# Feed-forward tiles taken in pairs: four low-rank products on four row groups of TensorE, four PSUM banks in a ring

## The chip, the cores and the metric

The kernel runs on one core of a Trainium2 chip. The metric is the device time of one execution in microseconds (us). It works in float32 throughout the stage that is changed.

## The reference, cut to what matters

The kernel computes four blocks on `x` (8 sequences of 100 tokens, width 512), each added to `x`: an alignment of `x` with a context, a mixture of 16 experts, a cross-attention, and a feed-forward block with low-rank experts. Only the last is touched:

```python
# x: (8, 100, 512), Wi: (2048, 512), Wo: (512, 2048), E = 4 experts of rank R = 4, TOP_K = 2
logits = einsum('bsd,ed->bse', x, Wg) + bg
scores = softmax(logits)
topv, topi = top_k(scores, 2)
w = sum(one_hot(topi, E) * topv[..., None], axis=-2)
base = einsum('bsd,fd->bsf', x, Wi)                 # shared by the experts
lora_low = einsum('bsd,erd->bser', x, A)            # 4 numbers for each expert
lora = einsum('bser,efr->bsef', lora_low, B)
h = relu(base[:, :, None, :] + lora)
out = einsum('bse,bsed->bsd', w, einsum('bsef,df->bsed', h, Wo))
```

For each token only its two best experts count, so the kernel forms, for each of 2048 hidden features, `w1*relu(base + lora1) + w2*relu(base + lora2)` and multiplies that by `Wo` once.

## The kernel before, in words

The five engines run their own instruction streams, written out by hand; semaphores (`wait_ge`, `then_inc`) are all that orders them. The last stage is `feed_forward` (from L1939).

**Tiles.** The 800 tokens are two halves of `NT4` = 400 columns, the 2048 features are `FJ` = 16 blocks of 128. A tile `i` of 32 is one block of features for one half: `g, f = i // FJ, i % FJ`. It has one PSUM bank of a ring of three (`bank[i % 3]`). Four more banks (`acc`) hold the output of a half, 512 features x 400 tokens, over 16 tiles. The eighth bank, `bx`, takes the logits at first, and later transposed outputs.

**A tile's steps.**
- `base_x(i)` (L2060): four matmuls of 128x128 weights by 400 columns put `Wi x` into the bank.
- `base(i)` (L2084): a matmul with only 16 contraction rows (partitions 0 to 15 of `Bt` and `lowT`) adds the best expert's low-rank term. `low` holds, for each token, the 16 numbers of `lora_low` with those of other experts set to zero.
- `weigh(i, 0)` on VectorE (L2201): relu of the bank, times the first weight `wb[0]`, into `h1`; it increments `read1`.
- `second(i)` (L2090): waits for `read1` and adds, in the same bank, a product of 16 rows at partitions 32 to 47. Those rows hold the second expert minus the first, so the bank now has the second expert's value.
- `weigh(i, 1)`: relu times `wb[1]` into `h2`; it increments `read2`, which also frees the bank.
- GpSimd adds `h1` and `h2` into `hs` (L2004), and increments `hs_ok`.
- `down(i)` (L2100): waits for `hs_ok`, then four matmuls of 128x128 weights `WoT` by 400 columns add to the four `acc` banks.

**TensorE's order (L2117 to L2129).** Iteration `i` issues `base_x(i)`, `base(i)`, `second(i-1)`, `down(i-2)`. The first three `base_x` are issued ahead of the loop (L2064). When half 0 is done, ScalarE and VectorE copy `acc` to `outT`, and iterations 18 to 21 end with `turn_back` of a sequence each (four transposes into `bx`, L2113). VectorE's `finish` adds that to `x` (L2211), and SyncE stores it. The last four sequences follow the loop.

**Ahead of the loop.** LayerNorm, transposes of `x` (L2037), logits (L2045, the first waits for semaphore `w_in` to reach 64: all small loads, `Bt` among them), softmax and top-2 on VectorE, `low` (L2173), whose completion is `low_ok`. TensorE issues `base_x(0..2)`, then waits for `low_ok`, transposes `low` (L2068), VectorE copies it to `lowT` (L2179), and four products of `ones` with diagonals of weights (L2076) spread the weights over the partitions (`wb`, L2183). The loop waits for all of that. SyncE issues the loads in the order `WgA`, `bg`, `Bt` twice, `Wi`, `WoT` (L1982 to L1987).

Of the kernel before, what the change touches and what calls it, by code (L numbers as in the profile page):

```python
# [9 lines left out]
ALU = mybir.AluOpType  # L10
# [3 lines left out]
B, S, D = 8, 100, 512  # L14
C = 722
P = 128
# [1922 lines left out]
def feed_forward(nc, io, res):  # L1939

    ctx = ExitStack()
    with ctx:
        sb, pb, sem = allocator(nc, ctx)
        x_sb, ident, ones = res["x"], res["ident"], res["ones"]
        Wi, WoT = res["Wmem"][:, :].rearrange("p (k f) -> p k f", f=F), sb("WoT", [P, FJ, D])
        Bt = sb("Bt", [2 * 32, F])
        WgA = sb("WgA", [P, KD, E_L + ER])
        bg = sb("bg", [S, E_L])
        stats, mv, rstd = sb("stats_f", [S, B, 6]), sb("mv_f", [S, B, 2]), sb("rstd_f", [S, B])
# [5 lines left out]
        top, topi, topf = sb("top_f", [S, B, 8]), sb("topi_f", [S, B, 8], U32), sb("topf_f", [S, B, 8])  # L1955
        iota_e = sb("iota_f", [S, E_L])
        hot = [sb(f"hot_f{k}", [S, B, E_L]) for k in range(2)]
        low = sb("low_f", [S, B, 64])
        lowT = sb("lowT", [64, XT])
        wdiag = [sb(f"wdiag{i}", [S, B // 2, S]) for i in range(2)]  # L1960
        wb = [sb(f"wb{k}", [P, XT]) for k in range(2)]
        NT4 = XT // 2
        h1 = [sb(f"h1_{i}", [P, NT4]) for i in range(2)]
        h2 = [sb(f"h2_{i}", [P, NT4]) for i in range(2)]
        hs = [sb(f"hs{i}", [P, NT4]) for i in range(3)]
        outT = [sb(f"outT{k}", [P, NT4]) for k in range(KD)]
        NBK = 3
        bank = [pb(f"bf{i}", [P, 512]) for i in range(NBK)]
        acc = [pb(f"acc{i}", [P, 512]) for i in range(4)]
        bx = pb("bx", [P, 512])  # L1970
        turned = [bx] * 4 + bank + [bx]
        w_in, wi_in, wo_in = sem("wf_in"), sem("wi_in"), sem("wo_in")
        (var_ok, root_ok, xn_ok, t_mm, t_ok, l_mm, sub_ok, exp_ok, low_ok, lt_mm, lt_ok, rep_ok, wb_mm, wb_ok, cs,
         base_mm, read1, d_mm, read2, hs_ok, acc_mm, acc_rd, out_s) = (sem("f_" + n) for n in (
# [56 lines left out]
        def _(pe):  # L2031
# [25 lines left out]
            def base_x(i):  # L2057
                g, f = i // FJ, i % FJ
                for k in range(KD):
                    pe.matmul(bank[i % NBK][:, 0:NT4], Wi[:, k, f * P:(f + 1) * P], xT[:, k, g * NT4:(g + 1) * NT4], start=k == 0, stop=False)  # L2060


            pe.wait_ge(wi_in, 16)
            for i in range(NBK):  # L2064
                base_x(i)
            pe.wait_ge(low_ok, 1)
            for b in range(B):
                ins = pe.transpose(acc[b // 4][0:64, (b % 4) * S:(b % 4 + 1) * S], low[:, b, :], ident[0:S, 0:S])  # L2068
                if b % 4 == 3:
                    ins.then_inc(lt_mm, 1)  # L2070
            for i in range(4):
# [6 lines left out]

            def base(i):
                g, f = i // FJ, i % FJ  # L2080
                if i >= NBK:
                    pe.wait_ge(read2, i - NBK + 1)
                    base_x(i)
                pe.matmul(bank[i % NBK][:, 0:NT4], Bt[0:ER, f * P:(f + 1) * P], lowT[0:ER, g * NT4:(g + 1) * NT4], start=False, stop=True).then_inc(base_mm, 1)  # L2084

            def second(i):

                g, f = i // FJ, i % FJ
                pe.wait_ge(read1, i + 1)
                pe.matmul(bank[i % NBK][:, 0:NT4], Bt[32:32 + ER, f * P:(f + 1) * P], lowT[32:32 + ER, g * NT4:(g + 1) * NT4],  # L2090
                          start=False, stop=True, skip_group_check=True).then_inc(d_mm, 1)

            def down(i):
                g, f = i // FJ, i % FJ
                pe.wait_ge(hs_ok, i + 1)
                if g and f == 0:
                    pe.wait_ge(kept_act, 2)
                    pe.wait_ge(kept_dve, 2)
                for k in range(KD):
                    ins = pe.matmul(acc[k][:, 0:NT4], WoT[:, f, k * P:(k + 1) * P], hs[i % 3][:, :], start=f == 0, stop=f == FJ - 1)  # L2100
# [15 lines left out]
            n = 2 * FJ  # L2116
            for i in range(n + 2):  # L2117
                if i < n:
                    base(i)
                if 1 <= i <= n:  # L2120
                    second(i - 1)
                if i == 2:
                    pe.wait_ge(wo_in, 16)
                if i >= 2:
                    down(i - 2)
                if FJ + 2 <= i < FJ + 6:
                    turn_back(i - FJ - 2)
            for b in range(4, B):
                turn_back(b)  # L2129

        @block.vector
        def _(dve):
# [14 lines left out]
            dve.wait_ge(w_in, 64)  # L2147
# [22 lines left out]
            link(dve.tensor_tensor(hot[1][:, :, :], hot[1][:, :, :], hot[0][:, :, :], ALU.subtract))  # L2170
            for b in range(B):
                for k in range(2):
                    ins = dve.tensor_tensor(low[:, b, 32 * k:32 * k + ER].rearrange("p (e r) -> p e r", r=R_L),  # L2173
                                            lga[:, b, E_L:E_L + ER].rearrange("p (e r) -> p e r", r=R_L),
                                            hot[k][:, b, :].unsqueeze(2).broadcast_to([S, E_L, R_L]), ALU.mult)
            ins.then_inc(low_ok, 1)
            for g in range(2):
                dve.wait_ge(lt_mm, g + 1)
                dve.tensor_copy(lowT[:, g * NT4:(g + 1) * NT4], acc[g][0:64, 0:NT4]).then_inc(lt_ok, 1)  # L2179

            def keep_weights(q):
                dve.wait_ge(wb_mm, q + 1)
# [13 lines left out]
            def weigh(i, k):  # L2196
                g = i // FJ
                dve.wait_ge((base_mm, d_mm)[k], i + 1)
                if i >= 2:
                    dve.wait_ge(hs_ok, i - 1)  # L2200
                dve.scalar_tensor_tensor((h1, h2)[k][i % 2][:, :], bank[i % NBK][:, 0:NT4], 0.0, wb[k][:, g * NT4:(g + 1) * NT4],  # L2201
                                         ALU.max, ALU.mult).then_inc((read1, read2)[k], 1)

            def keep_out(g):
# [8 lines left out]
            n = 2 * FJ  # L2213
            for i in range(n):
                weigh(i, 0)
                if i:
                    weigh(i - 1, 1)
                if i == FJ + 1:
                    keep_out(0)
                if FJ + 2 <= i < FJ + 6:  # L2220
                    finish(i - FJ - 2)
            weigh(n - 1, 1)
            keep_out(1)
            for b in range(4, B):
                finish(b)
# [93 lines left out]
```

## Time and profile before

| | us |
|---|---|
| median of 3 runs | 1273.11 (1272.48 to 1273.22) |
| the profiled execution, its own time | 1273.05 |
| its span in the trace | 1271.4 |
| TensorE matmul busy | 1090.3 (86%) |
| VectorE busy | 468.3 (37%) |
| ScalarE busy | 340.4 (27%) |
| GpSimd busy | 208.9 (16%) |

The profile is of one execution. "PE" is TensorE's matmuls, "PEld" its weight loads, which overlap them; DVE is VectorE, ACT ScalarE, POOL GpSimd, SP SyncE. A float32 matmul leaves two matmul records and two weight loads, so a group of 256 records is 128 matmuls of the code. Durations of neighbouring matmuls overlap: what one costs is read from the distance between the starts.

### The profile page before, as it was taken

Reading aid. Unit: us, or ns where it says so; the run is one execution under the profiler, and the core shown is the slowest. Engines: PE = TensorE matmul, PEld = TensorE weight load, DVE = VectorE, ACT = ScalarE, POOL = GpSimd, SP = SyncE. Lnnn points to the kernel's source line nnn. Section 1 sums busy time; section 2 is a strip of 40 time slices with the busy share of each in tenths; the row PEclk is TensorE's granted clock in tenths of the full one; section 3 lists DMA queues with packets and bytes.
Section 4 is the critical chain, followed back from the end, with each engine's and each line's share of the span. In section 5 each row is a group of like instructions: output and inputs, shape, how many; then the busy total and the mean of one; then the engine's idle time right before and its main releaser. Section 6 shows DMA issues by size and latency. Waiting matters only on the chain. (4 is left out here: it accounts for less than half of the span.)

```text
span 1271.4 us, 16885 instructions
## 1 busy us (share of the span) xinstructions
PE 1090.3 (86%) x5214; PEld 691.4 (54%) x5215; DVE 468.3 (37%) x1700; ACT 340.4 (27%) x804; POOL 208.9 (16%) x315
## 2 busy tenths in 40 slices
PE   5776679946937999999999999498999689999997
PEld 4773234522435777767677777244466364555553
DVE  4746888883560000000000000366455352112212
ACT  4323765770001222222222222223355210000000
POOL 0834031110021221212112112000000001111111
PEclk9897899967957999999999999698999967999999
DMA  8579004128305566776595655600000060000000
GB/s 287 141 164 270 8 1 168 56 93 236 117 13 191 179 199 200 263 259 205 197 320 173 181 173 170 188 8 1 0 2 1 16 261 1 1 1 7 20 1 26
DMA packets 76424, 152.52 MB, mean 120 GB/s; under 512 B 17691, under 2 KB 21915, under 8 KB 75567
## 3 DMA queue, kind: packets, MB, share of 16 engines
q1 hardware_dynamic: 63294, 130.95, 30.2%
q0 software_dynamic: 6928, 17.04, 6.1%
q10 hardware_dynamic: 6144, 3.84, 1.4%
q8 instruction: 27, 0.44, 0.1%
q14 instruction: 31, 0.25, 0.1%
HBM read 131.57 MB, written 20.25 MB: 119 GB/s over the span
## 5 line engine op out<-in xcount | busy, mean ns | idle before, releaser
L1269 ACT ACTIVATE att<-phid,b 128x128 f32<-128x128 f32 x216 | 79.4, 368 | 307.9 <-PE phid L1238 307.9
L1291 DVE TENSOR_TENSOR att<-py,att 128x512 f32<-128x512 f32 x27 | 18.7, 692 | 369.2 <-PE py L1246 369.2
L1238 PEld LDWEIGHTS phid<-tiles,W 128*128 128x128 f32 x896 | 111.5, 192 | 37.4 <-issue 37.4
L1238 PEld LDWEIGHTS phid<-tiles,Wmem 128*128 128x128 f32 x832 | 105.5, 195 | 38.9 <-issue 38.9
L1238 PE MATMUL phid<-tiles,W 128*128 x896 | 114.4, 276 | 1.2 <-issue 0.5
L1238 PE MATMUL phid<-tiles,Wmem 128*128 x832 | 108.3, 279 | 5.5 <-issue 4.5
L1246 PE MATMUL py<-W,att 128*128 128x512 f32 x224 | 110.0, 593 | 0.0
L1246 PE MATMUL py<-Wmem,att 128*128 128x512 f32 x208 | 102.2, 593 | 0.0
L2100 PE MATMUL acc<-hs,WoT 128*128 128x400 f32 x256 | 96.3, 521 | 0.5 <-POOL hs L2004 0.5
L2060 PE MATMUL bf<-xT_f,Wmem 128*128 128x400 f32 x256 | 93.2, 509 | 0.0
L2201 DVE SCALAR_TENSOR_TENSOR h<-bf,wb 128x400 f32<-128x400 f32 x64 | 34.0, 570 | 152.4 <-PE bf L2084 148.0
L2100 PEld LDWEIGHTS acc<-hs,WoT 128*128 128x128 f32 x256 | 47.1, 193 | 48.3 <-issue 20.8
L2060 PEld LDWEIGHTS bf<-xT_f,Wmem 128*128 128x128 f32 x256 | 49.4, 195 | 37.0 <-issue 2.2
L2004 POOL TENSOR_TENSOR hs<-h 128x400 f32<-128x400 f32 x32 | 33.0, 1031 | 210.8 <-DVE h L2201 210.8
L1313 POOL DMA_INDIRECT sum_d<-att,to_row x27 | 43.1, 1596 | 143.7 <-DVE att L1294 143.7
L995 PE MATMUL px<-ctx_rows,cost_mem 128*100 128x512 f32 (+1 forms) x96 | 44.7, 618 | 20.6 <-DVE cost_mem L1053 20.6
L2028 ACT COPY outT<-acc 128x400 f32<-128x400 f32 x4 | 1.8, 495 | 221.9 <-PE acc L2100 221.9
L1418 PE MATMUL ba<-lnT,Wmem 128*128 128x400 f32 x128 | 48.6, 525 | 5.6 <-DVE qT L1624 3.2
L858 DVE TENSOR_TENSOR_SCAN cost_mem<-reach_mem,cost_mem,enter 128x93 bf16<-128x93 bf16 x115 | 47.3, 411 | 11.8
L1621 DVE RECIPROCAL inv<-inv 128x400 f32<-128x400 f32 x16 | 42.4, 2652 | 19.7 <-ACT inv L1548 19.3
L1246 PEld LDWEIGHTS py<-W,att 128*128 128x128 f32 x224 | 36.1, 192 | 13.4 <-issue 13.4
L197 POOL TENSOR_SCALAR Wmem<-slots_row,pos_k 128x128 bf16<-128x128 f32 x48 | 39.7, 847 | 21.5 <-DVE pos_k L132 21.5
(364 smaller groups left out, 1655.1 us busy)
## 6 DMA issues: line engine op xcount, KB each, us to landing
Wmem<-in_W SPq DMA_DIRECT2D x16, 2048.0 KB, 14.0
W<-in_W SPq DMA_DIRECT2D x16, 2048.0 KB, 9.2
cT<-in_ctxT SPq DMA_DIRECT2D x8, 1444.0 KB, 11.7
ctx_rows<-in_ctx SPq DMA_DIRECT2D x8, 1280.0 KB
Wmem<-in_Wkv SPq DMA_DIRECT2D x2, 2048.0 KB, 9.2
att<-in_b SPq DMA_DIRECT2D x16, 256.0 KB, 14.1
Wmem<-in_WiT SPq DMA_DIRECT2D x1, 4096.0 KB
WoT<-in_WoT SPq DMA_DIRECT2D x1, 4096.0 KB
```

The costliest lines, as they stand in the source:

```text
L197: pool.tensor_scalar(sel[:, b, t, :], slots_row[:, :], pos[:, t, b:b + 1], None, ALU.is_equal)
L858: dve.tensor_tensor_scan(walk[:, q, 1:NO], code[:, q, :], enter[:, :], walk[:, q, 0:1], ALU.mult, ALU.max).then_inc(scanned_r, 1)
L995: ins = pe.matmul(px[b % 2][:, :], pathf[0:r, b % NPF * CT + t, :], ctx_rows[0:r, b * CT + t, :], start=t == 0, stop=t == CT - 1)
L1238: ins = pe.matmul(ph[j % NH][:, :], W1[u][:, k, j * P:(j + 1) * P], xgT[:, bass.ds(w, 1), k * P:(k + 1) * P].rearrange("p o t -> p (o t)") ...
L1246: ins = pe.matmul(py[:, :], hT[:, j - 2, :], W2[u][:, j - 2, :], start=j == 2, stop=j == HJ + 1)
L1269: act.activation(hT[:, j, :], ph[j % NH][:, :], ACT.Relu, bias=b1[:, bass.ds((e + u) * HJ + j, 1)]).then_inc(relu_ok, 1)
L1313: pool.indirect_dma_start(out=res["sum_d"], out_offset=bass.IndirectOffsetOnAxis(ap=to_row[:, 0:1], axis=0), in_=y[:, :], in_offset=None, ...
L1418: ins = pe.matmul(qk_b[j % 3][:, 0:NH2], w, lnT[:, k, g * NH2:(g + 1) * NH2], start=k == 0, stop=k == KD - 1)
L1621: link(dve.reciprocal(inv[j % 2][:, :], inv[j % 2][:, :]))
L2060: pe.matmul(bank[i % NBK][:, 0:NT4], Wi[:, k, f * P:(f + 1) * P], xT[:, k, g * NT4:(g + 1) * NT4], start=k == 0, stop=False)
L2100: ins = pe.matmul(acc[k][:, 0:NT4], WoT[:, f, k * P:(k + 1) * P], hs[i % 3][:, :], start=f == 0, stop=f == FJ - 1)
L2201: dve.scalar_tensor_tensor((h1, h2)[k][i % 2][:, :], bank[i % NBK][:, 0:NT4], 0.0, wb[k][:, g * NT4:(g + 1) * NT4], ALU.max, ALU.mult).the ...
```

## The change

Tiles are taken two at a time. Iteration `q` of 18 issues `base_x` of tiles 2q and 2q+1, then four products of 16 rows in a row: `base(2q)`, `base(2q+1)`, `second(2q-2)`, `second(2q-1)`, then `down(2q-4)`, a `turn_back` in iterations 10 to 13, and `down(2q-3)`. An even tile uses partitions 0 and 32 of `Bt` and `lowT`, an odd one 64 and 96, so `Bt`, `low` and `lowT` have four copies of the 16 rows. The ring of banks has four; the fourth is the former `bx`, so `base_x(3)` is issued after `low_ok`, and `turn_back` borrows the ring bank that `weigh(2q-2, 1)` has just read. `h1` and `hs` get four buffers.

```diff
-        Bt = sb("Bt", [2 * 32, F])
+        Bt = sb("Bt", [P, F])
-        low = sb("low_f", [S, B, 64])
-        lowT = sb("lowT", [64, XT])
+        low = sb("low_f", [S, B, P])
+        lowT = sb("lowT", [P, XT])
-        NBK = 3
+        NBK, NPAIR = 4, FJ
+        BACK_AT = FJ // 2 + 2
-        bx = pb("bx", [P, 512])
-        turned = [bx] * 4 + bank + [bx]
+        bx = bank[NBK - 1]
+        turned = [bank[2 * (BACK_AT + b - 1) % NBK] for b in range(B // 2)] + bank
...
-            for i in range(2):
+            for i in range(4):
                 sp.dma_start(Bt[32 * i:32 * i + ER, :], io["Bt"]).then_inc(w_in, 16)
...
-                if i >= 3:
-                    pool.wait_ge(acc_mm, i - 2)
-                pool.tensor_tensor(hs[i % 3][:, :], h1[i % 2][:, :], h2[i % 2][:, :], ALU.add).then_inc(hs_ok, 1)
+                if i >= 4:
+                    pool.wait_ge(acc_mm, i - 3)
+                pool.tensor_tensor(hs[i % 4][:, :], h1[i % 4][:, :], h2[i % 2][:, :], ALU.add).then_inc(hs_ok, 1)
...
-                    pe.wait_ge(w_in, 64)
+                    pe.wait_ge(w_in, 96)
...
-            for i in range(NBK):
+            for i in range(NBK - 1):
                 base_x(i)
             pe.wait_ge(low_ok, 1)
+            base_x(NBK - 1)
             for b in range(B):
-                ins = pe.transpose(acc[b // 4][0:64, (b % 4) * S:(b % 4 + 1) * S], low[:, b, :], ident[0:S, 0:S])
+                ins = pe.transpose(acc[b // 4][:, (b % 4) * S:(b % 4 + 1) * S], low[:, b, :], ident[0:S, 0:S])
...
             def base(i):
                 g, f = i // FJ, i % FJ
-                if i >= NBK:
-                    pe.wait_ge(read2, i - NBK + 1)
-                    base_x(i)
-                pe.matmul(bank[i % NBK][:, 0:NT4], Bt[0:ER, f * P:(f + 1) * P], lowT[0:ER, ...], ...).then_inc(base_mm, 1)
+                r = 64 * (i % 2)
+                pe.matmul(bank[i % NBK][:, 0:NT4], Bt[r:r + ER, f * P:(f + 1) * P], lowT[r:r + ER, ...], ...).then_inc(base_mm, 1)
             def second(i):
+                r = 64 * (i % 2) + 32
                 pe.wait_ge(read1, i + 1)
-                pe.matmul(..., Bt[32:32 + ER, ...], lowT[32:32 + ER, ...], ...).then_inc(d_mm, 1)
+                pe.matmul(..., Bt[r:r + ER, ...], lowT[r:r + ER, ...], ...).then_inc(d_mm, 1)
...
-                if b in (1, 2, 3):
-                    pe.wait_ge(acc_rd, b)
-                if b == B - 1:
-                    pe.wait_ge(acc_rd, 4)
+                if b < B // 2:
+                    pe.wait_ge(read2, 2 * (BACK_AT + b - 1) + 1)
+                if b == B // 2:
+                    pe.wait_ge(acc_rd, B // 2)
...
+            for q in range(NPAIR + 2):
+                pair = (2 * q, 2 * q + 1)
+                if 2 <= q < NPAIR:
+                    if 0 <= q - 1 - BACK_AT < B // 2:
+                        pe.wait_ge(acc_rd, q - BACK_AT)
+                    for i in pair:
+                        pe.wait_ge(read2, i - NBK + 1)
+                        base_x(i)
+                if q < NPAIR:
+                    for i in pair:
+                        base(i)
+                if 1 <= q <= NPAIR:
+                    for i in pair:
+                        second(i - 2)
+                if q == 2:
+                    pe.wait_ge(wo_in, 16)
+                if q >= 2:
+                    down(2 * q - 4)
+                    if 0 <= q - BACK_AT < B // 2:
+                        turn_back(q - BACK_AT)
+                    down(2 * q - 3)
...
             def weigh(i, k):
-                if i >= 2:
-                    dve.wait_ge(hs_ok, i - 1)
+                if i >= (4, 2)[k]:
+                    dve.wait_ge(hs_ok, i - (3, 1)[k])
...
+            for q in range(NPAIR + 1):
+                if q:
+                    weigh(2 * q - 2, 1)
+                    weigh(2 * q - 1, 1)
+                if q < NPAIR:
+                    weigh(2 * q, 0)
+                    weigh(2 * q + 1, 0)
+                if q == BACK_AT - 1:
+                    keep_out(0)
+                if 0 <= q - BACK_AT < B // 2:
+                    finish(q - BACK_AT)
```

The loop's old body, which the last two groups of lines replace, is at L2116 to L2127 and L2213 to L2222. The operations that build `low` on VectorE stay 16, and each now writes 32 numbers for a token, not 16.

## Rows read from the trace of the kernel before

**Rows 1.** The page: busy time of each engine, and TensorE's granted clock in 40 slices.

```profile
PE 1090.3 (86%) x5214; PEld 691.4 (54%) x5215; DVE 468.3 (37%) x1700; ACT 340.4 (27%) x804; POOL 208.9 (16%) x315
PEclk9897899967957999999999999698999967999999
```

**Rows 2.** Stretches: length, then PE, PEld, DVE, ACT, POOL busy, clock, DMA.

```profile
1072.71:1254.84 182.13, 182.13 (x577) 92.50 (x575) 33.38 (x62) 0.89 (x2) 28.87 (x28) 1.00 0.02 5
1052.00:1065.50 13.50, 12.30 (x20) 5.48 (x21) 4.68 (x9) 0.00 (x0) 2.05 (x2) 0.50 0.00 0
```

**Rows 3.** TensorE in order of time: start, us, line, operation. One tile of the loop.

```profile
1241.95 2.85 PE L2060 MATMUL bf<-xT_f,Wmem 128*128 128x400 f32 x8
1244.73 0.60 PE L2084 MATMUL bf<-lowT,Bt 16*128 16x400 f32 x1
1244.74 0.60 PE L2090 MATMUL bf<-lowT,Bt 16*128 16x400 f32 x1
1245.17 0.49 PE L2084 MATMUL bf<-lowT,Bt 16*128 16x400 f32 x1
1245.60 2.95 PE L2100 MATMUL acc<-hs,WoT 128*128 128x400 f32 x8
1248.39 2.85 PE L2060 MATMUL bf<-xT_f,Wmem 128*128 128x400 f32 x8
```

**Rows 4.** The same view: the end of the loop, and what follows.

```profile
1252.05 2.95 PE L2100 MATMUL acc<-hs,WoT 128*128 128x400 f32 x8
1254.93 0.93 PE L2090 MATMUL bf<-lowT,Bt 16*128 16x400 f32 x2
1255.79 5.64 PE L2100 MATMUL acc<-hs,WoT 128*128 128x400 f32 x16
1262.67 1.49 PE L2113 MATMUL bf<-ident,outT 128*100 128x128 f32 x12 [1.24 <-DVE outT L2207]
```

**Rows 5.** Groups by line from 1060 us on: busy, mean ns; idle before.

```profile
L2004 POOL TENSOR_TENSOR hs<-h 128x400 f32<-128x400 f32 x32 | 33.0, 1031 | 210.8 <-DVE h L2201 210.8
L2201 DVE SCALAR_TENSOR_TENSOR h<-bf,wb 128x400 f32<-128x400 f32 x62 | 32.8, 570 | 149.9 <-PE bf L2084 145.4 <-PE bf L2090 3.2 <-POOL hs L2004 1.2
```

**Rows 6.** All engines in order of time: a transposed sequence inside the loop.

```profile
1166.55 2.95 PE L2100 MATMUL acc<-hs,WoT 128*128 128x400 f32 x8
1169.34 0.60 PE L2113 MATMUL bx<-ident,outT 128*100 128x128 f32 x4
1169.78 2.85 PE L2060 MATMUL bf<-xT_f,Wmem 128*128 128x400 f32 x8
```

**Rows 7.** All engines in order of time: the start of the loop.

```profile
1055.41 3.03 PE L2084 MATMUL bf<-lowT,Bt 16*128 16x400 f32 x4 [0.67 <-DVE wb L2183]
1057.22 0.57 DVE L2201 SCALAR_TENSOR_TENSOR h<-bf,wb 128x400 f32<-128x400 f32 x1 [1.86 <-PE bf L2084]
1057.85 1.03 PE L2090 MATMUL bf<-lowT,Bt 16*128 16x400 f32 x1
1059.59 0.57 DVE L2201 SCALAR_TENSOR_TENSOR h<-bf,wb 128x400 f32<-128x400 f32 x1 [0.53 <-PE bf L2090]
1061.42 5.02 PE L2100 MATMUL acc<-hs,WoT 128*128 128x400 f32 x8 [0.54 <-POOL hs L2004]
1066.27 2.85 PE L2060 MATMUL bf<-xT_f,Wmem 128*128 128x400 f32 x8
```

**Rows 8.** All engines in order of time: ahead of the loop.

```profile
1037.24 10.54 PE L2060 MATMUL bf<-xT_f,Wmem 128*128 128x400 f32 x24
1042.11 1.46 DVE L2173 TENSOR_TENSOR low_f<-lga,hot_f 100x16 f32<-100x16 f32 x16
1047.61 0.85 PE L2068 MATMUL acc<-ident,low_f 100*64 100x100 f32 x8
```

**Rows 9.** The loads: SyncE's issue of `Bt`, and the wait that ended with it.

```profile
1014.05 1.20 SPq L1985 DMA_DIRECT2D Bt<-in_Bt  x2
PEld bx L2045 <- issue: 2.9, 1, 2.9
```

More of the change, by code:

```diff
@@ L1962, in feed_forward @@
         NT4 = XT // 2
-        h1 = [sb(f"h1_{i}", [P, NT4]) for i in range(2)]
+        h1 = [sb(f"h1_{i}", [P, NT4]) for i in range(4)]
         h2 = [sb(f"h2_{i}", [P, NT4]) for i in range(2)]
-        hs = [sb(f"hs{i}", [P, NT4]) for i in range(3)]
+        hs = [sb(f"hs{i}", [P, NT4]) for i in range(4)]
         outT = [sb(f"outT{k}", [P, NT4]) for k in range(KD)]
-        NBK = 3
+        NBK, NPAIR = 4, FJ
+        BACK_AT = FJ // 2 + 2
         bank = [pb(f"bf{i}", [P, 512]) for i in range(NBK)]
         acc = [pb(f"acc{i}", [P, 512]) for i in range(4)]
-        bx = pb("bx", [P, 512])
-        turned = [bx] * 4 + bank + [bx]
+        bx = bank[NBK - 1]
+        turned = [bank[2 * (BACK_AT + b - 1) % NBK] for b in range(B // 2)] + bank
         w_in, wi_in, wo_in = sem("wf_in"), sem("wi_in"), sem("wo_in")
@@ L2080, in base @@
                 g, f = i // FJ, i % FJ
-                if i >= NBK:
-                    pe.wait_ge(read2, i - NBK + 1)
-                    base_x(i)
-                pe.matmul(bank[i % NBK][:, 0:NT4], Bt[0:ER, f * P:(f + 1) * P], lowT[0:ER, g * NT4:(g + 1) * NT4], start=False, stop=True).then_inc(base_mm, 1)
+                r = 64 * (i % 2)
+                pe.matmul(bank[i % NBK][:, 0:NT4], Bt[r:r + ER, f * P:(f + 1) * P], lowT[r:r + ER, g * NT4:(g + 1) * NT4],
+                          start=False, stop=True).then_inc(base_mm, 1)
             def second(i):
                 g, f = i // FJ, i % FJ
+                r = 64 * (i % 2) + 32
                 pe.wait_ge(read1, i + 1)
-                pe.matmul(bank[i % NBK][:, 0:NT4], Bt[32:32 + ER, f * P:(f + 1) * P], lowT[32:32 + ER, g * NT4:(g + 1) * NT4],
+                pe.matmul(bank[i % NBK][:, 0:NT4], Bt[r:r + ER, f * P:(f + 1) * P], lowT[r:r + ER, g * NT4:(g + 1) * NT4],
                           start=False, stop=True, skip_group_check=True).then_inc(d_mm, 1)
@@ L2099, in down @@
                 for k in range(KD):
-                    ins = pe.matmul(acc[k][:, 0:NT4], WoT[:, f, k * P:(k + 1) * P], hs[i % 3][:, :], start=f == 0, stop=f == FJ - 1)
+                    ins = pe.matmul(acc[k][:, 0:NT4], WoT[:, f, k * P:(k + 1) * P], hs[i % 4][:, :], start=f == 0, stop=f == FJ - 1)
                 ins.then_inc(acc_mm, 1)
@@ L2114, in turn_back @@
                 ins.then_inc(back_mm, 1)
[L2116 to L2122, printed above, removed]
-                    pe.wait_ge(wo_in, 16)
-                if i >= 2:
[L2125 to L2128, printed above, removed]
+            for q in range(NPAIR + 2):
[13 more added lines that the diff above has]
+                if q == 2:
+                    pe.wait_ge(wo_in, 16)
+                if q >= 2:
[3 more added lines that the diff above has]
+                    down(2 * q - 3)
+            for b in range(B // 2, B):
                 turn_back(b)
@@ L2146, in _ @@
             dve.wait_ge(l_mm, B)
-            dve.wait_ge(w_in, 64)
+            dve.wait_ge(w_in, 96)
             dve.wait_ge(cs, 3)
@@ L2172, in _ @@
                 for k in range(2):
-                    ins = dve.tensor_tensor(low[:, b, 32 * k:32 * k + ER].rearrange("p (e r) -> p e r", r=R_L),
-                                            lga[:, b, E_L:E_L + ER].rearrange("p (e r) -> p e r", r=R_L),
-                                            hot[k][:, b, :].unsqueeze(2).broadcast_to([S, E_L, R_L]), ALU.mult)
+                    ins = dve.tensor_tensor(low[:, b, :].rearrange("p (u k c) -> p u k c", u=2, k=2)[:, :, k, 0:ER].rearrange("p u (e r) -> p u e r", r=R_L),
+                                            lga[:, b, E_L:E_L + ER].rearrange("p (e r) -> p e r", r=R_L).unsqueeze(1).broadcast_to([S, 2, E_L, R_L]),
+                                            hot[k][:, b, :].unsqueeze(1).unsqueeze(3).broadcast_to([S, 2, E_L, R_L]), ALU.mult)
             ins.then_inc(low_ok, 1)
@@ L2178, in _ @@
                 dve.wait_ge(lt_mm, g + 1)
-                dve.tensor_copy(lowT[:, g * NT4:(g + 1) * NT4], acc[g][0:64, 0:NT4]).then_inc(lt_ok, 1)
+                dve.tensor_copy(lowT[:, g * NT4:(g + 1) * NT4], acc[g][:, 0:NT4]).then_inc(lt_ok, 1)
             def keep_weights(q):
@@ L2198, in weigh @@
                 dve.wait_ge((base_mm, d_mm)[k], i + 1)
-                if i >= 2:
-                    dve.wait_ge(hs_ok, i - 1)
-                dve.scalar_tensor_tensor((h1, h2)[k][i % 2][:, :], bank[i % NBK][:, 0:NT4], 0.0, wb[k][:, g * NT4:(g + 1) * NT4],
+                if i >= (4, 2)[k]:
+                    dve.wait_ge(hs_ok, i - (3, 1)[k])
+                dve.scalar_tensor_tensor((h1[i % 4], h2[i % 2])[k][:, :], bank[i % NBK][:, 0:NT4], 0.0, wb[k][:, g * NT4:(g + 1) * NT4],
                                          ALU.max, ALU.mult).then_inc((read1, read2)[k], 1)
@@ L2211, in finish @@
                 dve.tensor_tensor(x_sb[:, b, :], x_sb[:, b, :], turned[b][0:S, :], ALU.add).then_inc(acc_rd, 1)
[L2213 to L2218, printed above, removed]
+            for q in range(NPAIR + 1):
[6 more added lines that the diff above has]
+                if q == BACK_AT - 1:
                     keep_out(0)
-                if FJ + 2 <= i < FJ + 6:
-                    finish(i - FJ - 2)
-            weigh(n - 1, 1)
+                if 0 <= q - BACK_AT < B // 2:
+                    finish(q - BACK_AT)
             keep_out(1)
```

## The prediction

> **What bounds the kernel now.** I read the page first: TensorE is busy for 1090.3 of 1271.4 us, no other engine for more than 468.3 [rows 1]. That is an average over four stages, so I went to the stretch of the changed loop. From 1072.71 to 1254.84 us TensorE's matmuls cover all 182.13 us at a granted clock of 1.00 (the 2.4 GHz level), VectorE works 33.38, GpSimd 28.87 [rows 2]. Those two wait for TensorE: VectorE's two readings of a tile are 0.57 us each, GpSimd's sum is 1.03, and nearly all of their idle time ended with TensorE's product (145.4 of VectorE's 149.9 us) [rows 5]. So the loop lasts as long as TensorE's matmuls, and only what shortens TensorE's own sequence counts.
>
> Then I took one tile in order of time, by the distances between starts [rows 3]:
> - four `base_x` matmuls, 1241.95 to 1244.73: 2.78 us
> - the slot of the low-rank products, 1244.73 to 1245.60: 0.87
> - four `down` matmuls, 1245.60 to 1248.39: 2.79
>
> A tile is 6.44 us. In the slot `base(i)` and `second(i-1)` run at once: their first records start 0.01 us apart, though each has a second record 0.44 later. The end of the loop shows what one such product costs when it is alone: `second(31)` starts at 1254.93 and `down(30)` at 1255.79, 0.86 us [rows 4]. One product costs 0.86, two on two row groups 0.87. This pair of rows carries the forecast: the slot is paid per group of products, not per product. Before 1066.27 us the picture differs: TensorE waits for VectorE and GpSimd, and the clock is 0.50, the 1.2 GHz level, from 1052.0 to 1065.5 [rows 2, 7].
>
> **The change part by part.** The full-size matmuls stay as they are, 32 tiles of 4 + 4, and so do the eight `turn_back`. What differs:
>
> *Slots in the loop.* After its start (from `down(0)` on) the kernel before has 29 slots of 0.87 (tiles 3 to 31) and one of 0.86: 26.09 us. After its start (from `base_x(4)` on) the changed one has 14 slots of four products (q = 2 to 15) and one of two (q = 16). At 0.87 each that is 12.18 + 0.86 = 13.04. The gain is 13.05 us. No row shows four products in one slot. Lower bound of such a slot: 0.87, nothing added. Upper bound: four after each other, 4 x 0.86 = 3.44; two by two is 1.74. I take 0.89, by the nearest row: the second product added 0.01, so two more add 0.02. That costs 14 x 0.02 = 0.3.
>
> The row on this is the pair 0.86 against 0.87 [rows 3, 4]. The Trainium skill, TensorE: Matmul & The Clock Gate, section "Measured speedup vs the span model", speaks against it in part: four row tiles of 32 rows gave 3.07 times the speed of one after another, not four. By that an estimated slot is 4 x 0.86 / 3.07 = 1.12 us, 14 x 0.25 = 3.5 us more than 0.87 in each, and the sum would end at 1262.4 us. The trace does not bear that out for two products, and does not show four.
>
> The same page, "The cost: per-tile semaphore tail", puts some 26 ns on each increment, and a slot now has four where it had two. An estimate by it is 14 x 0.05 = 0.7 us more; the trace has the second product's increment within its 0.01 us. I stay with the row.
>
> *Start of the loop.* Before, from the first low-rank product (1055.41) to `down(0)` (1061.42) pass 6.01 us [rows 7]: products with waits for VectorE between them, then GpSimd. After, `base(0)` and `base(1)` run together, and both are ready after 1.81 us (1057.22 less 1055.41); VectorE reads `bank 0` and `bank 1`; `second(0)` starts 0.63 us after the first reading began (1057.85 less 1057.22), and VectorE can read its result 1.74 later (1059.59 less 1057.85), which takes 0.57 and frees bank 0. Sum: 1.81 + 0.63 + 1.74 + 0.57 = 4.75, some 4.8 with the wait's latency, and then `base_x(4)` starts; `base(2)` and `base(3)` lie beside. GpSimd's sum is off the path, as `down(0)` comes only after two `base_x` and a slot. Gain 1.2 us. If the latencies don't overlap so: 0; if the clock were high: up to 2.5.
>
> *base_x(3) moves* ahead of the loop, past the wait for `low_ok` and ahead of the transposes of `low`. `low` is ready at 1043.57 (1042.11 + 1.46), while TensorE is in `base_x(0..2)` until 1047.61 [rows 8], so the new place in the queue causes no wait; it moves the transposes, and with them `lowT`, the weights and the loop's start, by 2.78 us. The loop has one `base_x` less, 2.78. Net 0. The transposes write 128 partitions, not 64, with weight loads twice as wide: they take 0.85 now [rows 8]; I add 0.1, at most 0.85.
>
> *The clock.* `down(0)` takes from 1061.42 to 1066.27, 4.85 us in place of 2.79, at the lower level [rows 7]: 2.06 lost. After, `base_x(4)` starts there instead, equally behind a few us of sparse products, and I take the same loss. TensorE's idle time while the weights are spread is as long as before but 2.8 us later, so the fall and the rise of the clock may come elsewhere. The low stretch was 13.50 us [rows 2] with 4.85 of dense work in it; gone altogether it would give back 2 to 3 us, and as much again in dense work would cost 2.
>
> *Edits I cost at nothing.* VectorE's 16 operations for `low` double in size; they took 1.46 us and have 4.04 of cover (1043.57 to 1047.61) [rows 8]; uncovered at most 1.46. The memset of `low` on GpSimd lies in some 24 us before it is needed. Two more loads of `Bt` stand ahead of `Wi` on SyncE's queue. The issue of two took 1.20 us, and the first logits wait for the loads: the weight loader's idle time before the logits, counted from the end of that wait, was 2.9 us [rows 9], the slack of the `Bt` loads. 1.2 to 1.8 later fits in it; without it the logits slip by at most 1.2. `Wi` and `WoT` follow 1.2 later, with `WoT` first needed 24 us after `base_x(0)`; were `Wi` late, the cost is those 1.2.
>
> *New waits in the loop.* Four readings of VectorE now follow each slot: 4 x 0.57 = 2.3 us, then two sums of GpSimd, 2.1. The bank for `base_x(2q)` is that of tile 2q-4, whose second reading is first in line behind slot q-1, done after some 0.6 us, while TensorE has two `down`, 5.58 us, ahead of it. The bank of 2q+1 follows by 0.6. `hs` has four buffers, and `down` comes 5.6 us and a slot after its sum. A `turn_back` adds 0.44 (1169.34 to 1169.78) before and after [rows 6]. Its new borrowed bank is read 0.6 us behind the slot, and the transposes start 2.79 behind it. `finish` holds the bank until some 3.9 us (2.79 + 0.44 + 0.69), and the next pair needs it at 6.0. Slack 2 us; without it up to 4 x 0.7 = 2.8 lost. Behind a waiting TensorE instruction stands everything, so any such miss is paid in full.
>
> *The tail* from `down(31)` on is the same work: copies, 16 transposes, additions, stores. 0.
>
> Sum: 13.05 + 1.2 - 0.3 - 0.1 = 13.85 us. The profiled execution took 1273.05 us (span 1271.4 and 1.65 around it), 0.06 below the median of 1273.11. Forecast: 1259.2 us, a span of 1257.55.
>
> **The rivals.**
> 1. *Four products only partly together*, some 1.12 us a slot. For: more weight loads and results in the same time than any row shows. Against: the second product's 0.01. 14 x (1.12 - 0.89) = 3.2 less gain: 1262.4 us. This is also what the page's factor gives.
> 2. *Two by two*, which is that the change does not do what it says: a slot of 1.74. For: each product has two records, and eight in flight are not seen. Against: a second record does not hold back the other product now. Slots 14 x 1.74 + 0.86 = 25.2, gain 0.9, with the start and the transposes 2.0: 1271.1 us, no change to tell.
> 3. *One after another.* If TensorE starts a product on a new row group only when the semaphore wait ahead of it has been passed with the array empty, a slot becomes 3.44: 14 x (3.44 - 0.89) = 35.7 more, and 1294.9 us, slower. It decides from a slot of 1.88 on (0.89 + 13.85 / 14). Against: `second` has such a wait now and starts within 0.01 us.
> 4. *Waits on the ring*: one stall in each pair at the bank or at `turn_back`. One of 0.2 us costs 3, 1262; 1 us in every pair would eat all of it. Slacks of 2 to 5 us speak against.
>
> **How the numbers follow.** Forecast 0.78; rival 1 0.09; rival 2 0.04; rival 3 0.03; rival 4 0.06. The forecast's own range is 1256.5 (clock low stretch gone) to 1261.5 (loads late, clock worse). With rivals 1 and most of 4 the range goes to 1263.5 and holds over 8 in 10. A measurement here tells 0.2%, 2.5 us. Faster by more: 0.92; within: 0.04; slower: 0.04.
>
> **What would show it.** In the profile after: four low-rank products that start within 0.05 us of each other, and 0.87 to 0.91 us from the first to `down`; a period of 12.03 us for a pair (2 x 5.57 + 0.89); `base_x(4)` some 4.8 us behind the first product; transposes of `low` at 1050.4; no idle time of TensorE before L2060 or L2113 of the kernel before, in the loop. The forecast is wrong if the slot is above 1.1, if a wait for `read2` or `acc_rd` appears on TensorE, or if the logits wait for `Bt`.

## The result, and the profile after

| | us |
|---|---|
| before, median | 1273.16 (1272.48 to 1274.41, 4 runs) |
| changed, median | 1256.20 (1254.46 to 1259.77, 4 runs) |
| ratio | 0.9869, 95% interval 0.9844 to 0.9895 |
| forecast | 1259.2 (1256.5 to 1263.5) |

The change is faster, as forecast, but by 17.0 us in place of 13.9, and the median lies 0.3 us below the range. The interval of the ratio stands for a gain of 13.4 to 19.9 us, so the medians of these runs alone do not tell by how much the forecast missed. Two later groups of runs of the same two kernels put the gain at 19.2 and 18.6 us, and the traces show where it comes from. The profiled execution took 1257.63 us, its span is 1255.0.

First TensorE in order of time in the changed kernel (start, us, line): a pair of tiles, then the end of the loop. A row group, below, is a block of 32 partitions of `Bt` and `lowT`; the four begin at 0, 32, 64 and 96. This answers to [rows 3, 4].

```profile
1071.06 0.60 PE L2084 MATMUL bf<-lowT,Bt 16*128 16x400 f32 x2
1071.08 0.60 PE L2092 MATMUL bf<-lowT,Bt 16*128 16x400 f32 x2
1071.50 0.50 PE L2084 MATMUL bf<-lowT,Bt 16*128 16x400 f32 x2
1071.52 0.50 PE L2092 MATMUL bf<-lowT,Bt 16*128 16x400 f32 x2
1071.95 5.64 PE L2102 MATMUL acc<-hs,WoT 128*128 128x400 f32 x16
1077.43 5.54 PE L2061 MATMUL bf<-xT_f,Wmem 128*128 128x400 f32 x16
1082.89 0.60 PE L2084 MATMUL bf<-lowT,Bt 16*128 16x400 f32 x2
...
1233.04 0.94 PE L2092 MATMUL bf<-lowT,Bt 16*128 16x400 f32 x4
1233.91 11.01 PE L2102 MATMUL acc<-hs,WoT 128*128 128x400 f32 x32
```

The slot with four products takes 0.89 us (1071.06 to 1071.95), as forecast. But the pair takes 11.83 us (1071.06 to 1082.89), not 12.03: two `down` are 5.48 and two `base_x` 5.46, where twice the durations of before make 5.58 and 5.56. The full-size matmuls did not stay as they were.

Now the way into the loop, all engines in order of time, which answers to [rows 7, 8].

```profile
1039.41 13.20 PE L2061 MATMUL bf<-xT_f,Wmem 128*128 128x400 f32 x32
1052.45 0.85 PE L2070 MATMUL acc<-ident,low_f 100*128 100x100 f32 x8
1056.67 1.91 PE L2078 MATMUL acc<-wdiag,ones 100*128 100x400 f32 x4 [0.48 <-DVE wdiag L2200]
1059.25 1.61 PE L2084 MATMUL bf<-lowT,Bt 16*128 16x400 f32 x8 [0.67 <-DVE wb L2194]
1063.29 7.85 PE L2061 MATMUL bf<-xT_f,Wmem 128*128 128x400 f32 x16 [0.18 <-DVE h L2212]
```

From the first low-rank product to `base_x(4)` pass 4.04 us, forecast 4.75. And the same stretches with their granted clock (last but two of the columns):

```profile
1045.00:1061.00 16.00, 13.48 (x48) 6.82 (x46) 6.90 (x22) 0.00 (x0) 0.00 (x0) 1.00 0.00 1
1061.50:1068.00 6.50, 6.32 (x12) 2.98 (x11) 2.02 (x4) 0.00 (x0) 2.02 (x2) 0.52 0.00 0
1071.06:1233.04 161.98, 161.98 (x561) 86.81 (x560) 32.07 (x62) 0.89 (x2) 28.34 (x28) 1.00 0.02 6
```

The clock stays at the 2.4 GHz level until about 1061, over the products that spread the weights and the first slot; before, it fell at 1052 and stayed low for 13.5 us [rows 2]. Now it is low for some 6.6, two thirds of that under `base_x(4)` and `base_x(5)`, which take 7.77 us (1063.29 to 1071.06) in place of 5.46.

Where the stage begins matters for the comparison. Its first VectorE operation started at 1013.13 us before and at 1015.30 after. The code ahead is the same, and in later profiles that operation falls between 1011.35 and 1016.14 whatever was edited behind it. So spans compare badly, and I use the length of the last stage, from that operation to the end of the span.

```profile
1013.13 1.29 DVE L2138 TENSOR_TENSOR x_res<-x_res,att 100x512 f32<-100x512 f32 x2 [4.47 <-PEq L45]
```

```profile
1015.30 1.29 DVE L2149 TENSOR_TENSOR x_res<-x_res,att 100x512 f32<-100x512 f32 x2 [4.56 <-PEq L45]
```

The first is of before: 1271.4 - 1013.13 = 258.27 us. The second is of after: 1255.0 - 1015.30 = 239.70. The stage gained 18.6 us where the forecast had 13.85. In this execution the stage began 2.2 us later than in that of before, which hides as much of the gain from the spans (16.4 us).

### The profile page after: what moved, and what is told of

The parts are those of the page before. It is cut to its first block and busy times, and to the rows that moved or that the text cites. A ratio compares the mean times of both kernels' runs of the same rounds, so it can differ in the third digit from the quotient of the medians.

```text
span 1255.0 us, 16888 instructions
## 1 busy us (share of the span) xinstructions
PE 1072.4 (85%) x5214; PEld 688.3 (55%) x5215; DVE 466.7 (37%) x1700; ACT 340.8 (27%) x804; POOL 208.2 (17%) x315
## 5 line engine op out<-in xcount | busy, mean ns | idle before, releaser
L2102 PE MATMUL acc<-hs,WoT 128*128 128x400 f32 x256 | 90.6, 505 | 0.0
L1246 PEld LDWEIGHTS py<-W,att 128*128 128x128 f32 x224 | 36.1, 192 | 13.4 <-issue 13.4
L825 DVE TENSOR_TENSOR_SCAN ctx_rows<-ctx_rows,cost_mem 128x46 f32<-128x46 f32 x115 | 37.3, 325 | 12.3 <-DVE ctx_rows L822 0.5
## 6 DMA issues: line engine op xcount, KB each, us to landing
att<-in_b SPq DMA_DIRECT2D x16, 256.0 KB, 14.1
```

The source lines that it names most:

```text
L825: dve.tensor_tensor_scan(reach[:, s + 1, 1:ROW], lower[:, s, :], cost[:, :, s], reach[:, s + 1, 0:1], ALU.min, ALU.add).then_inc(scanned, 1)
L1246: ins = pe.matmul(py[:, :], hT[:, j - 2, :], W2[u][:, j - 2, :], start=j == 2, stop=j == HJ + 1)
```

## The experiments

Of each profile I give the period of a pair of tiles and the length of the last stage ("stage"). The kernel before ran beside each group: 1274.41 us (`again`, `two_visits`, `two_groups`, `idle_fill`), 1274.66 (`no_lowrank`, `one_product`, `full_height`, `late_fourth`), 1275.56 (the last three). It was profiled once, at the start, so a stage of before is always 258.27. A visit is one passage of TensorE to the low-rank products and back. Its edges are the time that it adds to the full-height groups on its two sides, beside the slot itself. Full-height matmuls are those over all 128 contraction rows.

**The changed kernel again, unedited.**

> The changed kernel once more, nothing edited, to see what moves by itself. Every theory: a pair of tiles takes 11.83 us in the loop and a slot of four products 0.87 to 0.89, as in its first profile. The part from the last stage's first VectorE operation to the end is 239.7 us, within 0.3. If the times differ from each other by several us, the difference lies ahead of that stage.

1255.23 us; ratio 0.9856 (0.984 to 0.9873). The pair is 11.83, the stage 1250.5 - 1011.35 = 239.15. That is 0.55 less than in the first profile, more than the 0.3 expected: the four `base_x` ahead of the loop took 12.69 us in place of 13.04, and `base_x(4)` and `base_x(5)` 7.60 in place of 7.77, both with a part of them at the lower clock. The stage began 4 us earlier. So single executions differ by several us for reasons ahead of the stage, and the stage's length repeats to about 0.5.

**Two visits to the low-rank products.**

```diff
-                if q < NPAIR:
-                    for i in pair:
-                        base(i)
                 if 1 <= q <= NPAIR:
                     for i in pair:
                         second(i - 2)
...
                         turn_back(q - BACK_AT)
+                if q < NPAIR:
+                    for i in pair:
+                        base(i)
+                if q >= 2:
                     down(2 * q - 3)
```

> The four products of a pair of tiles are issued at two places: second, second, then down, then base, base, then down. All products, banks and waits stay. Theory A (each passage between full-height matmuls and products of 16 rows costs about 0.1 us beside the slot itself, so a slot costs 0.87 + 0.2): a pair takes 11.83 + 0.87 + 0.2 = 12.9 us, and the kernel 14 x 1.07 = 15 us more than the changed one, 1271. Theory B (the 0.2 us a pair that the change saved beyond the slot belong to the passages between base_x and down, which are also half as many): 11.83 + 0.87 = 12.7 us a pair, 12 us more, 1268.

1270.92 us (ratio to before 0.9977, 0.9967 to 0.9987). TensorE in order of time:

```profile
1079.43 5.54 PE L2061 MATMUL bf<-xT_f,Wmem 128*128 128x400 f32 x16
1084.90 0.94 PE L2092 MATMUL bf<-lowT,Bt 16*128 16x400 f32 x4
1085.77 2.95 PE L2102 MATMUL acc<-hs,WoT 128*128 128x400 f32 x8
1088.65 0.94 PE L2084 MATMUL bf<-lowT,Bt 16*128 16x400 f32 x4
1089.52 2.95 PE L2102 MATMUL acc<-hs,WoT 128*128 128x400 f32 x8
1092.31 5.54 PE L2061 MATMUL bf<-xT_f,Wmem 128*128 128x400 f32 x16
```

The pair takes 12.88 us (1079.43 to 1092.31), the figure of theory A and exactly the two tiles of before. The stage is 1270.6 - 1015.72 = 254.9. A `down` between two slots is 2.88 (1085.77 to 1088.65), one with a slot on one side 2.79: each side costs about 0.1. Putting the slots together is therefore worth 12.88 - 11.83 = 1.05 us a pair, not 0.87. All the rest of the change, in this kernel, is 3.5 us in the medians and 3.4 in the stage.

**Four products, two row groups.**

```diff
             def base(i):
-                r = 64 * (i % 2)
+                r = 0
             def second(i):
-                r = 64 * (i % 2) + 32
+                r = 32
```

> The odd tiles' products use the same two row groups as the even ones (rows 0 to 15 and 32 to 47), the order of everything stays: four products in one slot, but only two row groups. If the gain needs four groups, the slot has two rounds: 0.87 + 2 x 0.335 = 1.54 us (a second round without the edges) to 1.74 (two full slots), a pair 12.5 to 12.7 us, the kernel 9 to 12 us more than the changed one, 1265 to 1268. If being next to each other is all that counts, nothing changes: 11.83 us a pair, 1256.

1267.43 us (0.9942, 0.9925 to 0.9959).

```profile
1084.51 0.60 PE L2084 MATMUL bf<-lowT,Bt 16*128 16x400 f32 x1
1084.95 0.49 PE L2084 MATMUL bf<-lowT,Bt 16*128 16x400 f32 x1
1085.29 0.49 PE L2084 MATMUL bf<-lowT,Bt 16*128 16x400 f32 x1
1085.62 0.49 PE L2084 MATMUL bf<-lowT,Bt 16*128 16x400 f32 x1
1086.06 5.64 PE L2102 MATMUL acc<-hs,WoT 128*128 128x400 f32 x16
...
1097.01 0.60 PE L2084 MATMUL bf<-lowT,Bt 16*128 16x400 f32 x1
```

Left out above are the products of L2092, each 0.01 to 0.02 us behind one of L2084. The slot is 1.55 us (1084.51 to 1086.06), the pair 12.50, the stage 250.5. So there are two rounds, and the second costs 0.67: two records of 0.33, without edges. By the same figure 0.2 of a slot's 0.87 is not matmul time either. Of the 1.05 us a pair, 0.38 come from one visit in place of two, and 0.67 need the four row groups.

**No low-rank products from tile 4 on.** Both are left out, so this measures the slot with everything that hangs on it.

```diff
             def base_x(i):
-                    pe.matmul(..., start=k == 0, stop=False)
+                    ins = pe.matmul(..., start=k == 0, stop=i >= NBK and k == KD - 1)
+                if i >= NBK:
+                    ins.then_inc(base_mm, 1)
...
-                if q < NPAIR:
+                if q < 2:
                     for i in pair:
                         base(i)
-                if 1 <= q <= NPAIR:
+                if 1 <= q <= 2:
                     for i in pair:
                         second(i - 2)
...
-                dve.wait_ge((base_mm, d_mm)[k], i + 1)
+                dve.wait_ge(base_mm if i >= NBK else (base_mm, d_mm)[k], i + 1)
```

> Leaves out both low-rank products of tiles 4 to 31; the last base_x matmul signals in place of the first, and the second reading needs no product of its own. So the loop has 32 full-height matmul records... in each pair and no slot. Theory A (a slot costs 0.87 plus 0.2 at its edges): a record of a full-height matmul is 0.334 us, a pair 32 x 0.334 = 10.69, which is 1.14 less than the changed kernel's 11.83; the kernel 14 x 1.14 + 1.0 = 17 us less, 1239. Theory B (the 0.2 sits between base_x and down): 11.83 - 0.89 = 10.94 a pair, 13.3 less, 1243.

1240.33 us (2 runs; 0.9731, 0.9701 to 0.976). TensorE in order of time:

```profile
1076.67 5.54 PE L2061 MATMUL bf<-xT_f,Wmem 128*128 128x400 f32 x16
1082.05 5.54 PE L2104 MATMUL acc<-hs,WoT 128*128 128x400 f32 x16
1087.42 5.54 PE L2061 MATMUL bf<-xT_f,Wmem 128*128 128x400 f32 x16
```

A pair is 10.75 us: `base_x` 5.38 and `down` 5.37, with passages between them that cost nothing: behind the last slot of the changed kernel, too, 16 further records add 5.37 (11.01 - 5.64). Theory B's 10.94 is out. With a slot next to them the same groups take 5.46 and 5.48. A slot in all is 11.83 - 10.75 = 1.08 us: 0.89 itself, 0.08 in the group ahead of it, 0.11 in the group behind. The stage is 225.1, 14.1 to 14.6 less than the changed kernel's. The 17 expected had a slot at 1.14 us and 1.0 more on top.

**One product of the four.** Three of the four are left out from tile 4 on. The readings that lose their product are released as in the last run; only for even tiles does the last `base_x` matmul signal.

```diff
                 if q < NPAIR:
-                    for i in pair:
+                    for i in pair[0 if q < 2 else 1:]:
                         base(i)
```

> From tile 4 on, three of the four low-rank products of a pair are left out: only base(2q+1) stays. Theory A: the slot is paid for being entered, and three products more cost 0.02: a pair takes 11.81 us, and the kernel 1.0 less than the changed one (the slot behind the last pair is empty), 1255. If four products on four row groups share something (weight loads, results, increments), the pair falls by more: by 0.1 us for each 1.4 us of the whole.

1256.64 us (2 runs), and in its profile:

```profile
1083.49 0.93 PE L2086 MATMUL bf<-lowT,Bt 16*128 16x400 f32 x2
1084.36 5.64 PE L2104 MATMUL acc<-hs,WoT 128*128 128x400 f32 x16
1089.84 5.54 PE L2061 MATMUL bf<-xT_f,Wmem 128*128 128x400 f32 x16
1095.30 0.93 PE L2086 MATMUL bf<-lowT,Bt 16*128 16x400 f32 x2
```

The slot is 0.87 us, the pair 11.81. Three more products, with their weight loads, results and increments, cost 0.02 us together. The stage is 1254.1 - 1015.97 = 238.1, 1.0 to 1.6 less than the changed kernel's, where 1.0 was expected. The whole time does not show it, as differences ahead of the stage are larger.

**The products on the whole array.** From tile 4 on each takes 128 rows and weights from `Wi`, so other numbers are added.

```diff
+                if i >= NBK:
+                    w, l = Wi[:, 0, f * P:(f + 1) * P], lowT[:, g * NT4:(g + 1) * NT4]
...
```

The same stands in `second`.

> From tile 4 on, each low-rank product takes all 128 rows (weights from Wi, so its numbers are others), which puts it on the whole array like its neighbours: four matmuls of 0.67 us one after another, but no passage between two kinds. Theory A: 10.69 + 8 x 0.334 = 13.36 us a pair, 1.53 more than the changed kernel, 14 x 1.53 + 0.4 = 22 more in all, 1278. Theory B: 0.25 more a pair, 13.61, 1281.

1278.97 us (1.0034, 1.0023 to 1.0045). `base_x` groups start at 1077.96, 1091.39 and 1104.83:

```profile
1077.96 5.54 PE L2061 MATMUL bf<-xT_f,Wmem 128*128 128x400 f32 x16
1083.33 1.51 PE L2087 MATMUL bf<-lowT,Wmem 128*128 128x400 f32 x4
1084.68 1.51 PE L2098 MATMUL bf<-lowT,Wmem 128*128 128x400 f32 x4
1086.02 5.54 PE L2108 MATMUL acc<-hs,WoT 128*128 128x400 f32 x16
1091.39 5.54 PE L2061 MATMUL bf<-xT_f,Wmem 128*128 128x400 f32 x16
```

13.43 us a pair, that is 10.75 + 8 x 0.336: the same number of matmuls in the same places, and no edges anywhere. Theory A had 13.36, theory B 13.61. The stage is 261.9. The edge belongs to the change between the two kinds of matmul. Whether it is the 16 rows or the partitions they lie in was not tested apart.

What goes with the edge shows in the weight loads of the changed kernel:

```profile
1159.89 5.23 PEld L2061 LDWEIGHTS bf<-xT_f,Wmem 128*128 128x128 f32 x16
1160.22 5.54 PE L2061 MATMUL bf<-xT_f,Wmem 128*128 128x400 f32 x16
1165.69 0.19 PEld L2084 LDWEIGHTS bf<-lowT,Bt 16*128 16x128 f32 x2 [0.57 <-issue]
1165.69 0.60 PE L2084 MATMUL bf<-lowT,Bt 16*128 16x400 f32 x2
```

Between two full-height groups the first weights of the next are loaded 0.33 us ahead of its first matmul. At the change to the low-rank products they are loaded only when the first one starts, and the same holds on the way back (weights of `down` at 1166.57, its first matmul at 1166.58). No run tests whether this late load is the whole of the edge.

**base_x(3) back in the loop.**

```diff
             pe.wait_ge(low_ok, 1)
-            base_x(NBK - 1)
...
                 pair = (2 * q, 2 * q + 1)
+                if q == 1:
+                    base_x(NBK - 1)
```

In the expectation, the head is what stands ahead of the loop.

> base_x(3) is issued inside the loop (q = 1, after the first pair's products), as in the kernel before, not ahead of the transposes of low. The head is 2.7 us shorter, and TensorE idles over the spreading of the weights with less behind it. If the head's gain beyond the forecast came from the clock staying high for longer because base_x(3) stands there: the clock falls near 1052 as in the kernel before, the products for the weights take 2.9 us in place of 1.9, the first products and base_x(3) run at the lower level, and base_x(4) starts up to 3.5 us later than in the changed kernel: 1257 to 1260. If the clock has no part in it: base_x(4) starts 0.6 us earlier, as base_x(3) then fills a wait for VectorE, 1255.6.

1256.11 us (0.9853, 0.983 to 0.9877), against 1255.23 to 1256.99 for the changed kernel. Two rows, TensorE in time:

```profile
1054.76 3.00 PE L2077 MATMUL acc<-wdiag,ones 100*128 100x400 f32 x4 [0.48 <-DVE wdiag L2201]
1067.09 5.64 PE L2061 MATMUL bf<-xT_f,Wmem 128*128 128x400 f32 x16 [0.73 <-DVE h L2213]
```

Half right. The median lies between the two forecasts, near that of no part for the clock (1255.6). The clock does fall early, and those products take 3.00 us where the changed kernel has 1.91. `base_x(4)` starts 50.95 us into the stage (1067.09 - 1016.14), against 47.99. But the clock is back by then, and `base_x(4)` and `base_x(5)` take 5.57 us, not 7.77. The stage is 1256.5 - 1016.14 = 240.4, 0.7 to 1.2 more. I had priced the early fall and not the early rise.

**base_x(3) in the idle times behind the transposes.**

```diff
+            def base_x(i, ks=range(KD)):
...
             pe.wait_ge(low_ok, 1)
-            base_x(NBK - 1)
...
                     ins.then_inc(lt_mm, 1)
+            base_x(NBK - 1, (0, 1))
             for i in range(4):
...
                 pe.matmul(acc[(i + 2) % 4][:, 0:NT4], ones[0:S, :], ...).then_inc(wb_mm, 1)
+                if i in (1, 3):
+                    base_x(NBK - 1, (2 + i // 2,))
```

> The four matmuls of base_x(3), which stand ahead of the transposes of low, go into TensorE's idle times behind them: two right after the transposes (idle 1.28 us), one after the second and one after the fourth product that spreads the weights (idle 0.48 and 0.67). They cost 2.67 us ahead of the transposes now. If the loop's start hangs on the transposes of low as the chain of waits says: 2.4 us less, 1253.8, and up to 2.3 more if the clock then stays high through base_x(4) and base_x(5). Rival: the matmuls delay the products they stand ahead of, and the clock falls earlier, so that 1 us or less is left of it.

1250.92 us (0.9827, 0.9807 to 0.9846).

```profile
1048.09 1.53 PE L2061 MATMUL bf<-xT_f,Wmem 128*128 128x400 f32 x4
1049.54 1.61 PE L2078 MATMUL acc<-wdiag,ones 100*128 100x400 f32 x4
1050.98 0.84 PE L2061 MATMUL bf<-xT_f,Wmem 128*128 128x400 f32 x2
1051.66 1.87 PE L2078 MATMUL acc<-wdiag,ones 100*128 100x400 f32 x4
1053.36 0.84 PE L2061 MATMUL bf<-xT_f,Wmem 128*128 128x400 f32 x2
1054.19 1.61 PE L2086 MATMUL bf<-lowT,Bt 16*128 16x400 f32 x8
1057.47 5.64 PE L2061 MATMUL bf<-xT_f,Wmem 128*128 128x400 f32 x16 [0.19 <-DVE h L2214]
```

`base_x(4)` starts 45.07 us into the stage, 2.9 earlier, and in this execution the clock stayed at 1.00 from 1043 to 1241 us: the two `base_x` take 5.57. Stage 1246.9 - 1012.40 = 234.5.

Then both again, and the same move in the kernel before, for its `base_x(2)`.

> The changed kernel unedited, beside the next two, for the comparison with the best version. 1255.7 us, the mean of its two medians so far; last stage 239.2 to 239.7.

> The changed kernel with the four matmuls of base_x(3) in TensorE's idle times behind the transposes, once more. By its first profile the last stage takes 234.5 us, 4.7 to 5.2 less than unedited, with the granted clock at the upper level throughout. So 1250.8 us, 5 less than again5; if that was a lucky place of the clock's fall, the low stretch comes back in this profile, and 2.4 less is left, 1253.3.

> The kernel before, with the four matmuls of its base_x(2) moved in the same way, from ahead of the transposes of low to TensorE's idle times behind them. Pairs and four row groups are not in it. If the start's gain is one of filled idle time, and not of the pairs: 2.4 us less than the kernel before, and with the clock kept high through the first down (4.85 us at the lower level, 2.79 at the upper) and the first products up to 3 more: 1268.5 to 1271.5. If it takes the pairs, whose start waits less for VectorE: the clock still falls in the waits of the first three tiles, and 2.4 or less is left, 1272 and above. The period of two tiles stays 12.88 us by both.

| | median us | ratio to before | stage us |
|---|---|---|---|
| changed, unedited | 1256.99 | 0.9862 (0.9847 to 0.9877) | 239.3 |
| changed, base_x(3) in idle time | 1252.28 | 0.9812 (0.9799 to 0.9826) | 235.7 |
| before, base_x(2) in idle time | 1270.15 | 0.9959 (0.9945 to 0.9972) | 254.1 |

The best version is 4.7 us faster than the changed kernel, 23.3 faster than before. This time its clock did fall, and `base_x(4)` and `base_x(5)` took 7.27 us. So against the 239.3 of the unedited kernel the stage gains 3.5 us with the fall and 4.8 without it. Two profiles do not show what decides between the two. The kernel before gains 5.4 in the medians, 4.2 in the stage; in its profile:

```profile
1056.33 5.67 PE L2103 MATMUL acc<-hs,WoT 128*128 128x400 f32 x8 [1.20 <-POOL hs L2004]
1061.79 3.13 PE L2060 MATMUL bf<-xT_f,Wmem 128*128 128x400 f32 x8
```

`down(0)` starts 43.05 us into the stage, not 48.29, and then runs at the lower level: 5.46 us. The expectation had the clock high there and was wrong in that; the total lies within its range all the same. So this gain is one of idle time and clock, and the pairs are not needed for it.

## Why the prediction was wrong in size, point by point

**What bounds the kernel.** Right: in the changed loop TensorE's matmuls cover all of 161.98 us at 1.00.

**The slot.** Right: 0.89 us for four products, 0.87 for one. Rivals 1 to 3 fell, but their prices were wrong. They took 0.86 us for each product that has to wait for another, and that figure holds 0.2 that is paid once a visit. Two by two measured 1.55, not 1.74, and four after each other would be 0.87 + 3 x 0.67 = 2.88 by an estimate from the run on two row groups, not 3.44. That makes four together 3.2 times as fast. The Trainium skill (TensorE: Matmul & The Clock Gate, "Measured speedup vs the span model") has 3.07 for four row tiles, which is near. The 1.12 us that the prediction drew from it came of the 3.44. The same page's price of 26 ns for an increment ("The cost: per-tile semaphore tail") does not show in TensorE's own sequence: three products more with their increments cost 20 ns.

**"The full-size matmuls stay as they are."** This is the step that failed. In 2.78 and 2.79 us for eight records I had the price of the passages in and out of the slot: eight records alone are 2.69 (8 x 0.336), the rest is edge. The number was in the rows: behind the loop 16 records took 5.64 [rows 4] where eight took 2.95 [rows 3], 2.69 for the second eight. With half the slots, half the edges go: 15 slots in place of 30, at 0.19 us each (5.57 - 5.38), are 2.9 us. The traces have the same: from the end of `down(0)` to the end of the span before are 205.13 us, from the end of `base_x(5)` after 183.94. That is 21.19 less, where the forecast's terms give 18.32 (three `base_x` less, one `down` more, 12.77 for the slots). The Trainium skill has a rule (TensorEngine Tiling (Array Packing), "Key Properties"): a change of tiling mode drains TensorE. The runs agree in so far as each change costs, 0.2 us a slot beside the slot's own 0.87; the prediction gave it no term.

**Start of the loop.** 4.75 forecast, 4.04 measured. The sequence is the forecast one, but its terms were those of the lower clock, and `base(0)` and `base(1)` ran at the upper one: ready after 1.04 us, not 1.81. `second(0)` ran at the lower level and took its 1.74. 0.7 us.

**base_x(3) moved.** Net 0 forecast, with 0.1 for the transposes. The transposes took 0.85 us as before. The first low-rank product came 43.95 us into the stage (1059.25 - 1015.30), before 42.28 (1055.41 - 1013.13): 1.67 later, not 2.88. 1.0 of the 1.2 us is the clock: the second pair of products that spread the weights ran at the upper level. In all eight profiles with `base_x(3)` ahead of the transposes it takes 1.90 or 1.91 us. In the two without it (before, and `base_x(3)` back in the loop) it takes 2.92 and 3.00. The other 0.2 are `base_x(3)` itself, 2.67 without edges, and the transposes.

**The clock.** 2.06 lost forecast, which makes 7.62 us for `base_x(4)` and `base_x(5)`; measured 7.77, and 5.46 later in the loop. 0.15 less gain. The forecast let the fall "come elsewhere" and did not follow where.

**Loads.** The conclusion held, its reason was misread. The first logits start 8.36 us into the stage before (1021.49 - 1013.13) and after (1023.66 - 1015.30), so the two further loads of `Bt` did not hold them. But the 2.9 us [rows 9] was not the slack of `Bt`: the same 2.9 stands there with four loads, and is the weight loader's idle time since the transposes. How late `Bt` may land is not shown.

**Waits on the ring, turn_back, tail.** Right. A `turn_back` adds 0.44, no wait for `read2` or `acc_rd` appears in the loop, and from the first of the last two `down` the tail is the same.

Together: 2.9 + 0.7 + 1.2 - 0.15 = 4.65 of the 4.7 us by which the stage beat the forecast. So 2.9 us are the edges, which had no term, and 1.6 a clock that fell later than the forecast had it; 0.2 are `base_x(3)` and the transposes. The forecast gave the low end of its range to a low stretch that is gone. The time came out there for other reasons: the low stretch was there, 6.6 us long. The first median moved less than the stage, 17.0, but the later groups have 19.2 and 18.6. What happens ahead of the stage, which begins up to 4.8 us earlier or later with the same code ahead of it, is not explained here.

## What to carry to other kernels

In this float32 loop, products with few contraction rows cost by the visit, not by the product: collect them until all four row groups are used, and count for a visit the slot and its two edges, here 1.08 us together. To price a group of matmuls, take the difference between a long run and a short one, not the distance between starts, which has the edges in it. And when TensorE waits for another engine's results ahead of a dense loop, put independent matmuls into those waits: it gained the idle time in both kernels here, and may keep the clock up.

## What the runs showed of the hardware

- Four products of 16 rows on four row groups take 0.89 us, one takes 0.87, four on two groups 1.55. A second round on the same row groups adds 0.67.
- A change between full-height matmuls and products of 16 rows costs about 0.1 us each way in the neighbouring group. A change between groups of full-height matmuls on different banks costs nothing (5.37 and 5.38 us for 16 records).
- Behind another full-height group, the first weights of a full-height group were loaded 0.33 us ahead of its first matmul (1159.89 and 1160.22). At a change to low-rank products or back they were loaded within 0.01 us of it (1165.69; 1166.57 and 1166.58).
- The granted clock fell after sparse work, and not always: the version with filled idle time kept 1.00 from 1043 to 1241 us in one profile and in the other fell under `base_x(4)` and `base_x(5)` (7.27 us in place of 5.57).
